# Quantised rows turned by VectorE and two transfers instead of TensorE, with each down product a tile later

## The chip, the cores and the metric

The kernel runs on one core of a Trainium2 chip. The metric is the device time of one execution in microseconds (us). TensorE is called PE in the profile, VectorE DVE, ScalarE ACT, GpSimd POOL and SyncE SP; PEld is PE's load of a stationary operand. Each engine works through its own instructions in order, and semaphores order the engines among each other.

## The reference, cut to what matters

A graph layer on 2500 nodes with 1024 features, followed by a feed-forward block whose rows and weights are quantised:

```
xn = layernorm(x)
x  = x + segment_sum((xn @ W)[src] * edge_weight, dst) + mix(xn)      # z of the kernel is x + mix(xn)
r  = layernorm(x)
x  = x + ffn(r)

ffn(r):  gate = silu(bitlinear(r, w_gate));  up = bitlinear(r, w_up)   # 1024 -> 512
         return bitlinear(gate * up, w_down)                           # 512 -> 1024
bitlinear(x, w) = act_quant(x) @ weight_quant(w).T
act_quant:    scale = 127 / max|row|;  clip(round(x * scale), -128, 127) / scale
weight_quant: scale = 1 / mean|w|;     clip(round(w * scale), -1, 1) / scale
```

The integers of a quantised row and the ternary weights are exact in bf16, so the feed-forward products are bf16 products, and the scales are multiplied in behind them.

## The kernel before, in words

The nodes lie in 20 tiles of 125 rows (`ROWS`, `TILES`). The early stages (layer norm, the mix branch, the dense adjacency matrix that GpSimd scatters in device memory, the support xn @ W) are not touched by the change. Two stages are.

**Aggregation** (PE from L1581, `sources` and `aggregate`). The sum over edges is a dense product A x S, done for a group of four node tiles at a time (`GROUPS` = 5 groups, `GT` = 4). All eight PSUM banks hold one group, two per tile. For each of 20 source tiles PE runs 24 products of 512 columns: each operand is split in a high and a low part, and three products are made of them (L366 to L368). ScalarE makes the high parts (L895, L898), VectorE the sum of the two halves of A and the low parts (L1215, L1220, L1222), in two pairs of buffers; SP loads the next slices of A when a buffer is free. A pair of sources is one turn of the loops (`high_of_pair`, `low_of_pair`).

While a group is summed, the group before it is finished in between: VectorE adds z (`add_z`), takes the rows' statistics, and quantises one tile in each of four consecutive pairs (`quantise_r`, L1257, in the work buffer `rc`, two halves used in turn). ScalarE turns the rounded values into bf16 integers (`integers`, L908), which before the change go to `rq16`, where all 20 tiles have a place. VectorE does not wait for that conversion until it needs the same half of `rc` again.

**Feed-forward** (PE from L1638). For each tile PE runs 16 products for gate and up (8 blocks of 128 features, each against 512 columns; `gate_up`, L1645), 4 transposes of the quantised hidden rows (`transpose_hidden`, L1658) and 8 down products (`down`, L1675). The gate and up products need the quantised rows with features on the partitions. Before the change PE makes this by 8 transposes per tile against an identity (`rows_across`, L1624), and ScalarE copies the result from PSUM to `rqT` (`transposed_x`, L942). For each tile ScalarE applies silu to the gate (L947), VectorE multiplies, finds the rows' largest value and rounds (`hidden`, L1319 to L1331), ScalarE makes integers (L953) and copies the transposed hidden rows from PSUM (L959), and VectorE adds the down product to the residual (`add_down`, L1345).

The order is written out by hand on each engine. `ffn_tile` of PE runs the gate and up products of tile t+1 with the hidden transposes of tile t among them, then the row transposes of tile t+2, then the down product of tile t. VectorE runs `hidden(t)` and then `add_down(t-1)`. The last group (tiles 16 to 19) is quantised inside this stage: its first half (`largest_r`) one tile ahead of those in `ROUNDED_AT` = (4, 6, 9, 12), its second (`round_r`) at them. SP loads r rows of the other 16 tiles back from device memory and writes the output.

Of the kernel before, what the change touches and what calls it, by code (L numbers as in the profile page):

```python
# [73 lines left out]
X_BANK = (0, 4)  # L74
# [29 lines left out]
def layer_kernel(nc, x, src, dst, edge_weight, W, Wq, bq, Wk, bk, Wv, bv, mix_w, w_gate, w_up, w_down, out):  # L104
# [8 lines left out]
    wT_d = nc.dram_tensor("ternary", (12, P, D), BF16).ap()  # L113

# [116 lines left out]
    rq16 = e3("rq16", [P, TILES, D], BF16)  # L231
# [4 lines left out]
    rqT = s6("rqT", [P, 2, KT, P], BF16)  # L236
# [29 lines left out]
    s_acc = sems("s_acc", GT)  # L266
# [47 lines left out]
    s_rtr = sems("s_rtr", 2)  # L314
# [98 lines left out]
    V_LOAD, V_TURN = KT, KT + 2  # L413

# [24 lines left out]
    def _(sp):  # L439
# [286 lines left out]
    def _(act):  # L726
# [181 lines left out]
        def integers(g, d):  # L908

            act.wait_ge(s_rq[d % 2], g * (GT // 2) + d // 2 + 1)  # L910
            nc.scalar.activation(rq16[0:ROWS, bass.ds(g * GT + d, 1), :].rearrange("p o n -> p (o n)"),
                                 rc[0:ROWS, d % 2, :], ACT.Identity, bias=neg_round[0:ROWS, :]).then_inc(s_rq16[d % 2], 1)
# [10 lines left out]
        with act.Fori(1, GROUPS) as g:  # L923
# [15 lines left out]
        def transposed_x(i, m, bank=6):  # L939
            act.wait_ge(s_rtr[i], m + 1)  # L940
            act.wait_ge(s_q[i], m)
            nc.scalar.activation(rqT[:, i, :, 0:ROWS], by_block(PS16[:, bank, :])[:, :, 0:ROWS], ACT.Copy).then_inc(s_rqT[i], 1)  # L942
# [7 lines left out]
        def ffn_tile(h, i):  # L950
# [4 lines left out]
            if h * 2 + i + 1 < TILES:  # L955
# [4 lines left out]
                                 PS16[:, 7, 0:512].rearrange("p (k n) -> p k n", k=4)[:, :, 0:ROWS],  # L960
                                 ACT.Copy).then_inc(s_xev[i], 1)
            if h * 2 + i + 3 < TILES:
                transposed_x(i, h + 1)

        nc.scalar.activation(norms[:, 7, 0:1], eps[:, :], ACT.Silu)
        transposed_x(0, 0, X_BANK[0])
        transposed_x(1, 0, X_BANK[1])
        act.wait_ge(s_fb, 1)
        silu_gate(0, 0, 0)
        for t in range(TILES):  # L970
# [3 lines left out]
            if t == TILES - 4:  # L974
                transposed_x(1, HALF - 1)
# [7 lines left out]
    def _(dve):  # L983
# [277 lines left out]
        def largest_r(g, d):  # L1261
# [3 lines left out]
            dve.wait_ge(s_rq16[i], g * (GT // 2) + d // 2)  # L1265
# [45 lines left out]
        def hidden(h, i, at=None):  # L1311

            t = h * 2 + i
            sc, hh = h_sc[0:ROWS, i if at is None else at, :], hid[0:ROWS, i, :]
# [18 lines left out]
        def add_down(t, bank=4):  # L1333

            h, i = divmod(t, 2)
            at = i if t + 1 < TILES else 2
# [22 lines left out]
        hidden(0, 0)  # L1359
# [14 lines left out]
        for t in range(TILES - GT - 2, TILES - 2):  # L1374
            hidden(t // 2, t % 2)
            add_down(t - 1)
        hidden(HALF - 1, 0)
        hidden(HALF - 1, 1, 2)
# [5 lines left out]
    def _(pe):  # L1384
# [196 lines left out]
        def sources(g, i, m, first, last_one, ends=False):  # L1581
# [5 lines left out]
            for d in ORDER:  # L1587
# [11 lines left out]
                if ends and d == ORDER[2]:  # L1599
                    for n in range(2):  # L1600
                        pe.wait_ge(s_rq16[n], (TILES - GT) // 2)
                    pe.wait_ge(s_r[ORDER[0]], GROUPS)
                    rows_across(0, 0, X_BANK[0])
            last.then_inc(s_pe5[i], 1)

        def aggregate(g, ends=False):
# [5 lines left out]
            for i in range(2):  # L1612
                sources(g, i, g * HALF + HALF - 1, False, i == 1, ends and i == 1)

        def transpose_x(t, i, m):
            if i == 0:
                pe.wait_ge(s_rqT[1], m)
            else:
                pe.wait_ge(s_rqT[0], m + 1)
            rows_across(t, i, 6)  # L1620

        def rows_across(t, i, bank):
            for k in range(KT):
                last = nc.tensor.transpose(PS16[:, bank, k * P:k * P + ROWS],  # L1624
                                           rq16[0:ROWS, bass.ds(t, 1), k * P:(k + 1) * P].rearrange("p o n -> p (o n)"),
                                           ident16[0:ROWS, 0:ROWS])
            last.then_inc(s_rtr[i], 1)

        aggregate(0)
        with pe.Fori(1, GROUPS - 1) as g:  # L1630
            aggregate(g)
        aggregate(GROUPS - 1, True)
# [5 lines left out]
        def gate_up(i, m, hidden_of=None):  # L1638
            pe.wait_ge(s_rqT[i], m + 1)
            pe.wait_ge(s_h[i], m)  # L1640
            for c in range(2):
                for k in range(KT):
                    if hidden_of is not None and c == 1 and k == KT // 2:
                        transpose_hidden(*hidden_of)
                    last = nc.tensor.matmul(PS[0:ROWS, 2 * i + c, :], rqT[:, i, k, 0:ROWS], wT[:, c, :, k * P:(k + 1) * P],  # L1645
# [83 lines left out]
```

## Time and profile before

| What | us |
|---|---|
| median of 3 runs (lowest, highest) | 1678.12 (1676.09, 1686.17) |
| the profiled execution | 1680.37 |
| its span, first to last instruction | 1678.6 |
| PE busy | 1653.2 (98%) |
| VectorE busy | 1095.4 (65%) |
| ScalarE busy | 519.1 (31%) |
| GpSimd busy | 588.5 (35%) |

The chain of waits that ended last has PE for 91% of the span, DMA for 5% and VectorE for 2%. The three aggregation product lines (L366 to L368, which also serve earlier stages) hold 23% each, the gate and up products (L1645) 4%, the down products (L1675) 2%, the transposes of quantised rows (L1624) 1%. The TensorE clock was granted at 0.998 of its full level over the span. Busy time of PE counts overlapping instructions once; how closely its products follow each other is read from start to start. Idle time of an engine off the chain costs nothing.

### The profile page before, as it was taken

The numbers are of one execution on the slowest core, as the hardware profiler recorded it, in microseconds if no ns is written. First come the engines' busy times: TensorE is split into PE (matmuls) and PEld (weight loads), VectorE is DVE, ScalarE is ACT, GpSimd is POOL, SyncE is SP. The second block draws the span as 40 slices with busy tenths as digits, with TensorE's granted clock in tenths as the row PEclk, the third lists the DMA queues.
The fourth block names the chain that finished last, engine by engine and source line by source line (L and its number), as shares of the span: only waits on it lengthen the run. The fifth ranks groups of instructions, "written<-read, shape, count | busy, mean of one in ns | idle before, by whom it ended". The sixth has DMA issues, their size and how long they took to land.

```text
span 1678.6 us, 23146 instructions
## 1 busy us (share of the span) xinstructions
PE 1653.2 (98%) x8036; PEld 1344.9 (80%) x8036; DVE 1095.4 (65%) x2548; ACT 519.1 (31%) x618; POOL 588.5 (35%) x392
## 2 busy tenths in 40 slices
PE   6999999999999999999999999999999999999998
PEld 5899999888888888888877777888788887887665
DVE  7866573576676876656666664476485674764886
ACT  4632210222222111114232222233333333332554
POOL 2011565777776777777677700000000000000000
PEclk9999999999999999999999999999999999999999
DMA  9999878655676755657877747345345345452454
GB/s 295 377 402 348 308 234 263 169 138 124 151 195 167 183 141 149 149 138 191 243 209 192 191 147 205 102 135 137 96 146 136 96 136 145 136 145 62 146 172 123
DMA packets 158003, 302.93 MB, mean 180 GB/s; under 512 B 60241, under 2 KB 95105, under 8 KB 157938
## 3 DMA queue, kind: packets, MB, share of 16 engines
q1 hardware_dynamic: 88302, 222.54, 42.2%
q0 software_dynamic: 61824, 52.62, 15.3%
q10 hardware_dynamic: 7812, 26.97, 5.3%
q8 instruction: 32, 0.52, 0.1%
q14 instruction: 33, 0.27, 0.1%
HBM read 202.88 MB, written 99.20 MB: 180 GB/s over the span
## 4 chain that ended last, share of the span: by engine, by line
PE 91%; DMA 5%; DVE 2%; issue 1%; ACT 1%; SPq 0%; DVEq 0%; ACTq 0%
PE PS L367 23%; PE PS L368 23%; PE PS L366 23%; PE PS L1408 4%; PE PS L1410 4%; PE PS L1409 4%; PE PS L1645 4%; DMA Aside<-A_dense 2%; PE PS L1675 2%; PE PS L1472 2%; DMA xnT<-XT 1%; DMA X<-in_x 1%; PE PS L1624 1%; DVE stats L995 1%; PE PS L1388 0%
## 5 line engine op out<-in xcount | busy, mean ns | idle before, releaser
L706 POOL DMA_INDIRECT A_dense<-wtot,cell x336 | 545.4, 1623 | 229.5 <-DMA A_dense<-wtot,cell 133.9
L367 PE MATMUL PS<-SH,AL 125*125 125x512 f32 x784 | 310.0, 395 | 0.0
L366 PE MATMUL PS<-SL,AH 125*125 125x512 f32 x784 | 308.4, 393 | 1.6 <-DVE AL L1222 1.4
L368 PE MATMUL PS<-SH,AH 125*125 125x512 f32 x784 | 309.8, 395 | 0.0
L366 PE MATMUL PS<-WL,xtH 128*125 128x512 f32 x640 | 252.9, 395 | 0.0
L367 PE MATMUL PS<-WH,xtL 128*125 128x512 f32 x640 | 252.0, 394 | 0.0
L368 PE MATMUL PS<-WH,xtH 128*125 128x512 f32 x640 | 251.6, 393 | 0.0
L1220 DVE TENSOR_TENSOR SL<-S,SH 125x1024 fp32r<-125x1024 f32 x98 | 119.9, 1223 | 166.1 <-ACT SH L895 166.1
L895 ACT ACTIVATE SH<-S 125x1024 fp32r (+1 forms) x98 | 103.9, 1061 | 316.4 <-PE PS L368 316.3
L366 PEld LDWEIGHTS PS<-SL,AH 125*125 125x125 f32 x784 | 145.9, 186 | 39.8 <-DVE AL L1222 3.1
L367 PEld LDWEIGHTS PS<-SH,AL 125*125 125x125 f32 x784 | 146.1, 186 | 36.0
L368 PEld LDWEIGHTS PS<-SH,AH 125*125 125x125 f32 x784 | 145.5, 186 | 34.5
L378 DVE SCALAR_TENSOR_TENSOR junk<-keyrow,key,ewrow 128x256 bf16<-128x256 f32 x336 | 149.0, 480 | 2.1 <-DMA ewrow<-weight_rows 1.8
L368 PEld LDWEIGHTS PS<-WH,xtH 128*125 128x125 f32 x640 | 118.9, 186 | 28.8
L366 PEld LDWEIGHTS PS<-WL,xtH 128*125 128x125 f32 x640 | 118.9, 186 | 28.4
L367 PEld LDWEIGHTS PS<-WH,xtL 128*125 128x125 f32 x640 | 119.0, 186 | 28.0
L366 PE MATMUL PS<-TL,xtH 128*125 128x512 f32 x320 | 126.7, 396 | 0.0
L367 PE MATMUL PS<-TH,xtL 128*125 128x512 f32 x320 | 126.7, 396 | 0.0
L368 PE MATMUL PS<-TH,xtH 128*125 128x512 f32 x320 | 126.2, 394 | 0.0
L1120 DVE TENSOR_TENSOR xtL<-xt,xtH 128x1000 fp32r<-128x1000 f32 x60 | 71.9, 1198 | 71.5 <-ACT xtH L826 71.2
L691 POOL DMA_DIRECT2D A_dense<-zeros x40 | 46.6, 1165 | 143.5 <-PE PS L1410 83.2
L1408 PE MATMUL PS<-ring 125*128 125x512 f32 (+4 forms) x260 | 90.3, 347 | 5.2 <-DVE ring L1012 5.2
(190 smaller groups left out, 2547.9 us busy)
## 6 DMA issues: line engine op xcount, KB each, us to landing
A_dense<-zeros POOLq DMA_DIRECT2D x40, 1280.0 KB, 8.3
xt<-xnT SPq DMA_DIRECT2D x60, 500.0 KB, 6.1
Araw<-A_dense SPq DMA_DIRECT2D x100, 250.0 KB, 2.7
Aside<-A_dense SPq DMA_DIRECT2D x100, 250.0 KB, 2.9
keyrow<-key_rows SPq DMA_DIRECT2D x42, 512.0 KB, 4.1
ewrow<-weight_rows SPq DMA_DIRECT2D x42, 512.0 KB, 5.6
xnT<-XT ACTq DMA_DIRECT2D x20, 500.0 KB, 10.2
zx<-in_x SPq DMA_DIRECT2D x20, 448.0 KB
```

The lines of the kernel that those rows point to most:

```text
L366: nc.tensor.matmul(o, lh, rl, start=start, stop=False)
L367: nc.tensor.matmul(o, ll, rh, start=False, stop=False)
L368: return nc.tensor.matmul(o, lh, rh, start=False, stop=stop)
L378: nc.vector.scalar_tensor_tensor(junk[:, slot, 2 * c:2 * c + 2, :].rearrange("p a n -> p (a n)"), row, key[:, col], wrow, ALU.is_equal, AL ...
L706: pool.indirect_dma_start(cells[m], bass.IndirectOffsetOnAxis(cell[:, col:col + 1], 0), wtot[:, col:col + 1], None, compute_op=ALU.add).th ...
L895: nc.scalar.activation(sh, S[0:ROWS, bass.ds(s, 1), :].rearrange("p o n -> p (o n)"), ACT.Copy).then_inc(s_s[i], 1)
L1120: nc.vector.tensor_tensor(xtL[i][:, :, :], xt[:, i], xtH[i][:, :, :].bitcast(F32), ALU.subtract).then_inc(s_xtl[i], 1)
L1220: nc.vector.tensor_tensor(sl, S[0:ROWS, bass.ds(s, 1), :].rearrange("p o n -> p (o n)"), sh.bitcast(F32), ALU.subtract)
L1408: nc.tensor.matmul(o, hi[:, cols], rl, start=first and opens, stop=False, skip_group_check=True)
L1409: nc.tensor.matmul(o, lo[:, cols], rh, start=False, stop=False, skip_group_check=True)
L1410: last = nc.tensor.matmul(o, hi[:, cols], rh, start=False, stop=last_one, skip_group_check=True)
L1645: last = nc.tensor.matmul(PS[0:ROWS, 2 * i + c, :], rqT[:, i, k, 0:ROWS], wT[:, c, :, k * P:(k + 1) * P], start=k == 0, stop=k == KT - 1)
```

## The change

The bf16 integers of a tile are written to the first half of the work buffer `rc` itself (`integer_rows`). VectorE transposes them in blocks of 32x32 into the second half (`turn_rows`, `turned_rows`), writing with a step of 8 elements. Four DMAs store the result to a new array in device memory, so that features get on its rows (`store_turned`, runs of 256 elements), and one DMA fetches it into `rqT`, which now holds all 20 tiles (`fetch_rows`). The transposes by PE, their PSUM banks and the copies by ScalarE are gone. The stationary operand of the gate and up products is read with a step of 8 elements and has 128 columns in place of 125.

For the first four groups the turning lies in the aggregation: VectorE turns a tile after the pair of sources that follows its quantisation, ScalarE's queue issues the stores a pair later, ahead of that pair's conversion, and the fetches another pair later. The next quantisation into the same half of `rc` waits for the store (`s_rqst`). For the last group VectorE turns inside the feed-forward stage, and SP issues the transfers between the output's writes.

In the feed-forward stage PE now runs: gate and up products of tile t, hidden transposes of tile t-1, down product of tile t-2. VectorE runs `hidden(t)` and `add_down(t-2)`; the scales of the hidden rows have three places.

```diff
+    rqT_d = nc.dram_tensor("rqT", (TILES, P, D), BF16).ap()
...
-    rq16 = e3("rq16", [P, TILES, D], BF16)
+    rqT = e3("rqT", [P, TILES, D], BF16)
...
+    def store_turned(eng, dram, rows, sem):
+        for a in range(4):
+            eng.dma_start(dram.rearrange("(b i) (a f) -> a i b f", b=4, a=4)[a],
+                          rows[a * 32:(a + 1) * 32, :].rearrange("p (b f) -> p b f", b=4)).then_inc(sem, 16)
+
+    def integer_rows(i):
+        return rc[:, i, 0:D // 2].bitcast(BF16)
+
+    def turned_rows(i):
+        return rc[:, i, D // 2:D].bitcast(BF16)
+
+    def store_rows(eng, g, d):
+        eng.wait_ge(s_turn, g * GT + d + 1)
+        store_turned(eng, rqT_d[bass.ds(g * GT + d, 1)].rearrange("o p n -> (o p) n"), turned_rows(d % 2), s_rqst[d % 2])
+
+    def fetch_rows(eng, g, d):
+        eng.wait_ge(s_rqst[d % 2], 64 * (g * (GT // 2) + d // 2 + 1))
+        eng.dma_start(rqT[:, bass.ds(g * GT + d, 1), :].rearrange("p o n -> p (o n)"),
+                      rqT_d[bass.ds(g * GT + d, 1)].rearrange("o p n -> (o p) n")).then_inc(s_rqT[d % 2], 16)
...
# SP, feed-forward
-        with sp.Fori(0, (TILES - GT) // 2 - 1) as h:
-            for i in range(2):
-                write_rows(h * 2 + i, h, i)
-                load_r(h * 2 + i + 2, i)
-        for t in range(TILES - GT - 2, TILES - 1):
+        for i in range(2):
+            sp.wait_ge(s_rqT[i], 16 * (TILES - GT) // 2)
+        for t in range(TILES - 1):
             write_rows(t, t // 2, t % 2)
+            if t + 2 < TILES - GT:
+                load_r(t + 2, t % 2)
+            if t + 1 in ROUNDED_AT:
+                store_rows(sp, GROUPS - 1, ROUNDED_AT.index(t + 1))
+            if t in ROUNDED_AT:
+                fetch_rows(sp, GROUPS - 1, ROUNDED_AT.index(t))
...
# ACT, aggregation
             for d in range(GT):
                 high_of_pair(g, 2 + d)
+                if d >= 1:
+                    store_rows(act, g - 1, d - 1)
                 integers(g - 1, d)
+                if d >= 2:
+                    fetch_rows(act, g - 1, d - 2)
...
-            with act.Fori(2 + GT, HALF) as h:
+            high_of_pair(g, 2 + GT)
+            store_rows(act, g - 1, GT - 1)
+            fetch_rows(act, g - 1, GT - 2)
+            high_of_pair(g, 3 + GT)
+            fetch_rows(act, g - 1, GT - 1)
+            with act.Fori(4 + GT, HALF) as h:
                 high_of_pair(g, h)
...
# DVE
-            dve.wait_ge(s_rq16[i], g * (GT // 2) + d // 2)
+            dve.wait_ge(s_rqst[i], 64 * (g * (GT // 2) + d // 2))
...
+        def turn_rows(g, d):
+            dve.wait_ge(s_rq16[d % 2], g * (GT // 2) + d // 2 + 1)
+            nc.vector.transpose(turned_rows(d % 2).rearrange("p (b j k) -> p b k j", b=4, j=32),
+                                integer_rows(d % 2).rearrange("p (k b j) -> p b k j", b=4, j=32)).then_inc(s_turn, 1)
...
+        nc.vector.memset(rc[96:P, :, :], 0.0)
...
             for d in range(GT):
                 quantise_r(g - 1, d)
                 low_of_pair(g, 2 + d)
+                turn_rows(g - 1, d)
...
         for t in range(1, TILES - GT - 2):
-            hidden(t // 2, t % 2)
-            add_down(t - 1)
+            hidden(t)
+            if t >= 2:
+                add_down(t - 2)
+            if t - 1 in ROUNDED_AT:
+                turn_rows(GROUPS - 1, ROUNDED_AT.index(t - 1))
...
# PE, feed-forward (ffn_tile, transpose_x and rows_across are removed)
-                    last = nc.tensor.matmul(PS[0:ROWS, 2 * i + c, :], rqT[:, i, k, 0:ROWS], wT[:, c, :, k * P:(k + 1) * P],
+                    last = nc.tensor.matmul(PS[:, 2 * i + c, :], rows[:, :, k], wT[:, c, :, k * P:(k + 1) * P],
...
+        gate_up(0, 0)
+        pe.wait_ge(s_r[1], GROUPS)
+        gate_up(1, 0)
+        for d in (2, 3):
             pe.wait_ge(s_r[d], GROUPS)
...
+        transpose_hidden(0, 0)
+        with pe.Fori(1, HALF) as h:
+            gate_up(0, h)
+            transpose_hidden(h - 1, 1)
+            pe.wait_ge(s_z[1], HALF + h - 1)
+            down(h - 1, 0, 4, False)
+            gate_up(1, h)
+            transpose_hidden(h, 0)
+            pe.wait_ge(s_z[0], HALF + h)
+            down(h - 1, 1, 4, False)
```

## Rows read from the trace of the kernel before

**Rows 1.** Windows: one aggregation group and the feed-forward stage (span; busy us of each engine with its count; clock; DMA).
```profile
core 0: us, PE busy (x) PEld busy (x) DVE busy (x) ACT busy (x) POOL busy (x), PEclk, DMA share, GB/s
1326.00:1438.00 112.00, 111.77 (x483) 89.40 (x482) 72.55 (x103) 39.46 (x47) 0.00 (x0) 1.00 0.44 128
1551.00:1660.00 109.00, 107.68 (x667) 71.50 (x665) 90.88 (x184) 61.47 (x80) 0.00 (x0) 1.00 0.51 151
```
**Rows 2.** Chain of waits, one tile of the feed-forward stage (start us, us, what).
```profile
1638.20 0.44 PE PS L1624 x8
1638.65 1.73 PE PS L1675 x8
1640.38 2.59 PE PS L1645 x12
...
1644.06 0.44 PE PS L1624 x8
```
**Rows 3.** Timeline of PE, start of the feed-forward stage (start, us, line; idle before).
```profile
1553.15 6.21 PE L1645 MATMUL PS<-wT,rqT 128*125 128x512 bf16 x28
1560.68 0.40 PE L1658 MATMUL PS<-ident,hq 125*128 125x125 bf16 x4 [1.32 <-ACT hq L953]
```
**Rows 4.** Timeline of VectorE (DVE), start of the feed-forward stage.
```profile
1554.04 2.46 DVE L1243 BATCH_NORM_STATS2 stats<-zr 125x6 f32<-125x512 f32 x4
1556.98 0.75 DVE L1319 SCALAR_TENSOR_TENSOR hid<-PS,u_back,gate 125x512 f32<-125x512 f32 x1 [0.48 <-PE PS L1645]
...
1562.74 0.70 DVE L1319 SCALAR_TENSOR_TENSOR hid<-PS,u_back,gate 125x512 f32<-125x512 f32 x1
```
**Rows 5.** Timeline of VectorE, feed-forward tiles that also quantise a last-group tile.
```profile
1577.86 0.80 DVE L1266 TENSOR_SCALAR rc<-zr,group_mv,rstd 125x1024 f32<-125x1024 f32 x1
...
1579.83 0.74 DVE L1319 SCALAR_TENSOR_TENSOR hid<-PS,u_back,gate 125x512 f32<-125x512 f32 x1
...
1582.64 1.28 DVE L1345 SCALAR_TENSOR_TENSOR fin<-PS,h_sc,rt 125x1024 f32<-125x1024 f32 x1
1583.83 0.14 DVE L1276 TENSOR_SCALAR x_back<-f_sc 125x1 f32<-125x1 f32 x1
...
1585.72 0.74 DVE L1319 SCALAR_TENSOR_TENSOR hid<-PS,u_back,gate 125x512 f32<-125x512 f32 x1
```
**Rows 6.** Timelines of PE and VectorE, the last tile's gate and up products.
```profile
1661.03 4.48 PE L1645 MATMUL PS<-wT,rqT 128*125 128x512 bf16 x20
...
1666.41 0.75 DVE L1319 SCALAR_TENSOR_TENSOR hid<-PS,u_back,gate 125x512 f32<-125x512 f32 x1 [1.36 <-ACT gate L947]
```
**Rows 7.** Timeline of VectorE, one quantising pair of the aggregation.
```profile
1472.82 0.67 DVE L1222 TENSOR_TENSOR AL<-Araw,AH 125x500 fp32r<-125x500 f32 x1
...
1477.31 0.81 DVE L1266 TENSOR_SCALAR rc<-zr,group_mv,rstd 125x1024 f32<-125x1024 f32 x1
...
1481.39 0.68 DVE L1215 TENSOR_TENSOR Araw<-Araw,Aside 125x500 f32<-125x500 f32 x1
...
1483.12 0.67 DVE L1222 TENSOR_TENSOR AL<-Araw,AH 125x500 fp32r<-125x500 f32 x1
```
**Rows 8.** Timeline of ScalarE (ACT), the same pair.
```profile
1474.49 1.06 ACT L895 ACTIVATE SH<-S 125x1024 fp32r<-125x1024 f32 x1 [2.07 <-PE PS L368]
...
1475.96 1.14 ACT L911 ACTIVATE rq<-rc,neg_round 125x1024 f32 x1
...
1485.62 1.06 ACT L895 ACTIVATE SH<-S 125x1024 fp32r<-125x1024 f32 x1 [2.89 <-PE PS L368]
```
**Rows 9.** Groups by line and shape, 1551 to 1679 us (count, busy us, mean ns; idle before).
```profile
L1645 PEld LDWEIGHTS PS<-wT,rqT 128*125 128x125 bf16 x320 | 42.4, 138 | 22.0
L1624 PEld LDWEIGHTS PS<-ident,rq 125*128 125x128 bf16 x61 | 3.9, 97 | 1.5 <-issue 0.3
L1269 DVE TENSOR_REDUCE f_sc<-rc 125x1 f32<-125x1024 f32 x4 | 4.9, 1220 | 0.1
```
**Rows 10.** DMA issues on ScalarE (L100, ns min/median/max), and landing of the ternary weights' stores (L600).
```profile
L100 ACTq DMA_DIRECT2D r<-zr x4: 342/350/396, 1119.1 to 1453.8; - x4
DMA to landing us min/median/max: 2.0/3.5/4.4
```

More of the change, by code:

```diff
@@ L73 @@
 NORM_BANK = (5, 1)
-X_BANK = (0, 4)
 ROUNDED_AT = (4, 6, 9, 12)
@@ L265, in layer_kernel @@
     s_Azero = sems("s_Azero", 2)
-    s_acc = sems("s_acc", GT)
+    s_acc = {d: sem(f"s_acc{d}") for d in (0, 2, 3)}
     s_bd = sem("s_bd")
@@ L313, in layer_kernel @@
     s_rstd = sem("s_rstd")
-    s_rtr = sems("s_rtr", 2)
+    s_rqst = sems("s_rqst", 2)
+    s_turn = sem("s_turn")
     s_s = sems("s_s", 2)
@@ L1309, in scales_back, with hidden @@
                                     ALU.mult).then_inc(s_fb, 1)
-        def hidden(h, i, at=None):
-            t = h * 2 + i
-            sc, hh = h_sc[0:ROWS, i if at is None else at, :], hid[0:ROWS, i, :]
+        def hidden(t):
+            h, i = divmod(t, 2)
+            sc, hh = h_sc[0:ROWS, t % 3, :], hid[0:ROWS, i, :]
             n = t * 5
@@ L1358, in _ @@
         dve.wait_ge(s_fb, 1)
-        hidden(0, 0)
+        hidden(0)
         row_stats(GROUPS - 1, ORDER[2:])
@@ L1373, in _ @@
         dve.wait_ge(s_fb, 2)
[L1374 to L1378, printed above, removed]
+        for t in range(TILES - GT - 2, TILES - 1):
+            hidden(t)
+            add_down(t - 2)
+        hidden(TILES - 1)
         for t, bank in ((TILES - 3, 4), (TILES - 2, 0), (TILES - 1, 2)):
@@ L1579, in _, with sources @@
         pe.wait_ge(s_fc, 3)
-        def sources(g, i, m, first, last_one, ends=False):
+        def sources(g, i, m, first, last_one):
             pe.wait_ge(s_lo5[i], m + 1)
@@ L1598, in sources, with aggregate @@
                     last.then_inc(s_acc[d], 1)
[L1599 to L1603, printed above, removed]
             last.then_inc(s_pe5[i], 1)
-        def aggregate(g, ends=False):
+        def aggregate(g):
             for i in range(2):
@@ L1612, in aggregate, with gate_up @@
             for i in range(2):
[L1613 to L1627, printed above, removed]
+                sources(g, i, g * HALF + HALF - 1, False, i == 1)
         aggregate(0)
-        with pe.Fori(1, GROUPS - 1) as g:
+        with pe.Fori(1, GROUPS) as g:
             aggregate(g)
-        aggregate(GROUPS - 1, True)
         def down_blocks(c, k):
             return wT[:, 2, 2 * c:2 * c + 2, :].rearrange("p a (b n) -> p (a b) n", b=2)[:, :, k * P:(k + 1) * P]
-        def gate_up(i, m, hidden_of=None):
-            pe.wait_ge(s_rqT[i], m + 1)
+        def gate_up(i, m):
+            rows = rqT[:, bass.ds(m * 2 + i, 1), :].rearrange("p o (r k) -> p (o r) k", k=KT)
+            pe.wait_ge(s_rqT[i], 16 * m + 16)
             pe.wait_ge(s_h[i], m)
@@ L1652, in transpose_hidden @@
             pe.wait_ge(s_hq16[i], h + 1)
[L1653 to L1656 removed]
+            pe.wait_ge(s_xev[i], HALF + h)
             for k in range(INNER // P):
[L1658 removed]
+                last = nc.tensor.transpose(PS16[:, 6 + i, k * P:k * P + ROWS], hq16[0:ROWS, i, k * P:(k + 1) * P],
                                            ident16[0:ROWS, 0:ROWS])
             last.then_inc(s_xtr[i], 1)
[L1662 to L1669 removed]
         def down(h, i, bank, by_halves):
@@ L1679, in down @@
             last.then_inc(s_u[i], 1)
-        pe.wait_ge(s_r[2], GROUPS)
-        rows_across(1, 1, X_BANK[1])
         pe.wait_ge(s_wT, 64)
+        pe.wait_ge(s_r[0], GROUPS)
         gate_up(0, 0)
-        for d in (1, 3):
+        pe.wait_ge(s_r[1], GROUPS)
+        gate_up(1, 0)
+        for d in (2, 3):
             pe.wait_ge(s_r[d], GROUPS)
-        ffn_tile(0, 0)
-        ffn_tile(0, 1)
-        with pe.Fori(1, (TILES - GT - 2) // 2) as h:
-            for i in range(2):
-                ffn_tile(h, i)
-        for t in range(TILES - GT - 2, TILES - 3):
-            pe.wait_ge(s_rq16[t % 2], (t + 2) // 2 + 1)
-            ffn_tile(t // 2, t % 2)
-        pe.wait_ge(s_rq16[1], HALF)
-        transpose_x(TILES - 1, 1, HALF - 1)
-        gate_up(0, HALF - 1, (HALF - 2, 1))
-        gate_up(1, HALF - 1)
-        transpose_hidden(HALF - 1, 0)
-        pe.wait_ge(s_z[0], 2 * HALF - 1)
-        down(HALF - 2, 1, 4, False)
+        transpose_hidden(0, 0)
[8 more added lines that the diff above has]
+            down(h - 1, 1, 4, False)
         pe.wait_ge(s_h[0], HALF)
```

34 lines of the change are left out of this document (4 added, 30 removed).

## The prediction

> **What bounds the kernel now.** I read the busy time by stretch first. In the aggregation of four node tiles (the second to fifth group look alike) PE is busy for all of the 112 us shown and VectorE for 73; in the feed-forward stage PE is busy for 107.7 of 109 us, but VectorE for 90.9 [rows 1]. The clock is at its full level in both, so PE's time is work, and VectorE is the engine with little left. The chain of waits through the feed-forward stage then gives PE's tile: 8 transposes of the quantised rows (0.44 us), the down product (1.73), 12 of the 16 gate and up products (2.59), the transposes of the hidden rows and the last four products; one tile to the next is 5.86 us [rows 2]. The timelines of VectorE and ScalarE at the edges of that stage and in one quantising pair of the aggregation [rows 3 to 8] show what stands ready when.
>
> **Part 1: PE's transposes leave the feed-forward stage.** 20 tiles x 0.44 us = 8.7 us off a chain that PE holds [rows 2]. The tile becomes 5.42 us. ScalarE's 20 evictions of the transposed rows go too; it had idle time, so they are worth nothing here.
>
> **Part 2: the start of that stage.** Now PE waits 1.32 us for the first hidden rows, 3.70 us after their VectorE chain starts at 1556.98 [rows 3, 4]. With the transposes gone the first products start 0.44 us earlier, at 1552.26 on an unchanged aggregation, and the first two tiles' products run to 1559.18. The first hidden chain can start when the row statistics end (1556.50 less 0.44, 1556.06), so PE waits to 1559.76: 0.58 us. Then come the third tile's products (3.46 us, to 1563.4). The second hidden chain started 5.76 us after the first [rows 4], so at 1561.8, and its transposes can run at 1565.5: a wait of 2.1 us, which the old order filled with the first down product. 2.7 against 1.3: +1.4 us.
>
> **Part 3: VectorE in that stage.** From row to row, a tile's hidden chain is 2.81 us and the addition of the down product 1.19, the first half of a last-group tile's quantisation 1.97, the second 1.89; in the old stage such tiles follow each other without a gap, at 5.89 us [rows 5]. The change adds one block transpose of 128x1024 in each of four tiles (5, 7, 10, 13). No row shows one. Ends: nothing (the start-to-start floor), and 2.4 us, twice a full-width pass; I take 1.2 us, the duration of the reduction over the same 1024 columns [rows 9]. Tiles 5 to 13 then need 9 x 4.00 + 3 x 1.97 + 3 x 1.89 + 4 x 1.2 = 52.4 us against PE's 9 x 5.42 = 48.8: +3.6 us. The looser order (the down product a tile later) gives slack for one tile, but a queue that is full for nine cannot be outwaited; the quieter tiles from 14 on catch up only up to PE. At the ends of the range of the transpose this term is 4.8 less (that is, none) and 4.8 more.
>
> **Part 4: the end.** The last tile's hidden chain starts 0.9 us after its products end, behind ScalarE's activation [rows 6]. In the new order the chain of the tile ahead begins a tile earlier, so this activation can start with the first half of the products: -0.7 us. What follows is untouched. The addition of tile 16, now between the last two hidden chains, takes 1.19 us of a stretch in which VectorE waits.
>
> Feed-forward stage: -8.7 + 1.4 + 3.6 - 0.7 = -4.4 us.
>
> **Part 5: the aggregation pays.** 16 tiles are turned there, in four groups, with PE full. In the pair shown PE gives up a source's buffers at 1474.5 and needs the refill of the other pair of buffers at 1485.6; two sources are 11.13 us [rows 8]. VectorE ends that pair at 1477.31, quantises for 4.08 us, and has the next source ready at 1481.39 + 2.40 = 1483.8: 1.8 us early [rows 7]. Now ScalarE issues four stores ahead of the conversion to integers, at 0.35 us each [rows 10]; with 0.3 us of them beside the activation in front (my choice), conversion moves from 1475.96 to about 1477.1 and ends at 1478.2. VectorE, which used to go straight on, waits 0.9 us for it, then turns the rows to 1479.5. The next quantisation also waits until the turned rows of two tiles before are stored, since they lie in the buffer that it overwrites. Those stores go out up to 1477.1. A store of 256 KB to device memory took 2.0 to 4.4 us, 3.5 in the median [rows 10]; the last quarter is smaller, and I take 2.6: 1479.7. Then 4.08 + 2.40: ready at 1486.2, 0.6 us late. Two pairs per group are so (third and fourth tile): 8 x 0.6 = 4.8 us. Before the second tile no store stands in the way; the row has 1.0 us of slack there (ready at 1473.5 [rows 7], needed at 1474.5), and 1.2 us of turning and 0.1 of hand-off make it 0.3 us late: 1.2 us over four groups. Together +6.0 us. Ends: nothing, if half a microsecond more is hidden; and with stores that take the row's 4.4 us, 1.8 us more in eight pairs, +20.4.
>
> **Edits that I cost at nothing.** The fetches (one issue and 256 KB each) and the 10 MB in all: the 16 DMA engines are half idle in both stages [rows 1], and a fetched tile has tens of microseconds until PE reads it; if that cover is gone, a fetch of a last-group tile would hold PE at tile 16 or later. In the last stage stores and fetches go through SP behind the output's writes and ahead of the next ones: up to nine issues of 0.35 us, 3.2 us of a 5.4 us tile; the row loads have a full tile of lead. One clearing of 32 partitions of the work buffer falls in the aggregation's first group, where VectorE waits. The wider products (128 rows in place of 125) stream the same 512 columns.
>
> **Part 6: the stationary operand.** Its columns now lie 16 bytes apart. The load is 0.138 us for 125 packed columns, and 0.097 for the 128-column loads of the transposes [rows 9], under products that follow each other at 0.216 us (12 in 2.59 [rows 2]). I take no cost, as it may grow by 0.08 us unseen. A gain has no room either: the spacing is the product's.
>
> **Where a rule speaks against it.** The Trainium skill, "SBUF — State Buffer", on cachelines: accesses that touch a new 16-byte line each time pay a penalty, and 8 bf16 is just that stride. No run here shows its size. "TensorE: Matmul & The Clock Gate", on weight-path modes, says that loads of 128 non-fp32 columns are read faster, packed or strided; the 0.097 against 0.138 us agrees for packed ones.
>
> **Sum.** -4.4 + 6.0 = +1.6 us. The profiled execution took 1680.37 us for a span of 1678.6; it would become 1682.0. It stands 2.25 us above the median of 1678.12, so on the median's scale 1679.7.
>
> **Rivals.**
> 1. *The turning is hidden in the aggregation.* Stores land within 2 us or issues overlap more. For it: 1.8 us of slack in each quantising pair. Against: three additions in series on VectorE. Only the feed-forward sum is left: 1678.1 - 4.4 = 1673.7; with a transpose of 0.7 us, 1671.7. Chance 0.20.
> 2. *Slower: the strided weight load shows.* It decides in the 320 gate and up loads, once one exceeds 0.216 us. At twice today's 0.138 us: 320 x 0.060 = 19.2 us; PE then sets the pace again, so the 3.6 us of part 3 vanish: -8.7 + 1.4 - 0.7 + 19.2 + 6.0 = +17.2, 1695.3. At three times: 320 x 0.198 = 63.4, 1739.5. From 0.275 us on it is slower by over 1%. For it: no load of the trace is strided. Against: 0.08 us of room, and the wide load is the shorter. Chance 0.10. By the cacheline sentence above it would be this case.
> 3. *The block transpose takes 2.4 us.* In the feed-forward stage +4.8; in the aggregation the turn ends at 1480.7 instead of the store's 1479.7, 8 x 1.0 = 8.0, and 4 x 1.2 = 4.8: 1679.7 + 17.6 = 1697.3. Against: the reduction of this width is 1.2 us. Chance 0.12. ("VectorE: DVE Perf Modes" of the Trainium skill, on the three transpose paths, gives 311 ns for 128x128, an estimate of 2.5 us for eight; with a fixed part in it, it would be less.)
> 4. *Stores land late,* 4.4 us or more after issue: the +20.4 above in place of 6.0, 1694.1 and up. Chance 0.08.
>
> **How the numbers follow.** My forecast has 0.50 (its own range 1674 to 1686). A change of under 1% (16.8 us) cannot be told from none here. Faster by over 1% would need twice all that PE gives up: 0.02. Slower: nearly all of rival 2 past its point 0.07, half of 3 (0.06), most of 4 (0.05), 0.02 for what I don't see: 0.20. The rest, 0.78, is no change. The range runs from rival 1's lower time, 1671, to rival 3's, 1697; beyond lie the worse half of rival 2 and a tenth of the rest.
>
> **What would show it.** Feed-forward: no transposes of quantised rows, tile spacing of 5.4 us outside tiles 5 to 13 and near 5.8 within, a wait of 2 us at the second hidden transposes. Aggregation: PE waiting for the low part of A, 0.3 to 0.6 us, three times a group. The block transpose at 1.2 us, and the gate and up products still 0.216 us apart. Wrong, if the aggregation shows no wait or one over 1 us each, or if the products spread.

## The result: 3.6% slower, 1740.1 us against 1677.1

The kernel after takes 1740.1 us in the median of 4 runs (1736.49 to 1741.18), the kernel before, run beside it, 1677.11 (1675.54 to 1686.17). The ratio is 1.0359 with a 95% interval of 1.0324 to 1.0393. The forecast was 1679.7 us in a range of 1671 to 1697, so time and range both missed. The profiled execution took 1736.49 us.

Windows of both kernels show where it went: the first stretch runs from the aggregation's first product to the first gate and up product, the second from there to the end of the span. First before, then after (columns as in [rows 1]).

```profile
992.20:1553.20 561.00, 558.43 (x2418) 446.71 (x2417) 341.67 (x468) 188.78 (x227) 0.00 (x0) 1.00 0.44 128
1553.20:1678.60 125.40, 117.14 (x707) 76.58 (x704) 98.61 (x201) 64.87 (x86) 0.00 (x0) 0.99 0.50 148
```
```profile
987.70:1598.00 610.30, 573.70 (x2402) 453.34 (x2400) 416.31 (x484) 189.17 (x226) 0.00 (x0) 0.97 0.45 131
1598.00:1734.80 136.80, 115.96 (x561) 73.11 (x560) 116.98 (x206) 45.47 (x67) 0.00 (x0) 0.96 0.52 150
```

The aggregation is 49.3 us longer, the feed-forward stage 11.4 us, where it should have been shorter. VectorE is 75 and 18 us busier, PE has 37 and 21 us without work where it had 3 and 8, and the granted clock fell from 1.00 to 0.97 and 0.96. The page names what is new on VectorE:

```profile
L1309 DVE STREAM_TRANSPOSE rc<-rc 128x1024 bf16<-128x1024 bf16 x20 | 96.6, 4828 | 19.7 <-ACT rc L935 19.7
```

One block transpose takes 4.83 us; the prediction had 1.2, and 2.4 as its upper end. The timeline of VectorE in a quantising pair of after answers [rows 7] (L1244 was L1222, L1237 was L1215, L1288 was L1266). The columns are start, duration and what ran; in brackets the idle time before.

```profile
1388.11 0.68 DVE L1244 TENSOR_TENSOR AL<-Araw,AH 125x500 fp32r<-125x500 f32 x1
1390.37 4.83 DVE L1309 STREAM_TRANSPOSE rc<-rc 128x1024 bf16<-128x1024 bf16 x1 [1.59 <-ACT rc L935]
1394.82 0.89 DVE L1288 TENSOR_SCALAR rc<-zr,group_mv,rstd 125x1024 f32<-125x1024 f32 x1
...
1398.99 0.67 DVE L1237 TENSOR_TENSOR Araw<-Araw,Aside 125x500 f32<-125x500 f32 x1
```

Between the end of one pair's low parts (1388.8) and the start of the next (1399.0) lie 10.2 us; in [rows 7] they are 4.1. PE's timeline in the same place:

```profile
1386.52 0.50 PE L366 MATMUL PS<-SL,AH 125*125 125x512 f32 x1 [3.67 <-DVE AL L1244]
1386.86 0.39 PE L367 MATMUL PS<-SH,AL 125*125 125x512 f32 x1
...
1388.40 0.63 PE L367 MATMUL PS<-SH,AL 125*125 125x512 f32 x1
1388.83 0.63 PE L368 MATMUL PS<-SH,AH 125*125 125x512 f32 x1
...
1391.39 0.44 PE L368 MATMUL PS<-SH,AH 125*125 125x512 f32 x1
1391.67 0.40 PE L366 MATMUL PS<-SL,AH 125*125 125x512 f32 x1
```

PE waits 3.67 us for the low part of A. After that wait its products, 0.23 us apart at first, are 0.43 us apart from 1388.40 to 1391.39: these seven steps take 1.4 us more than at the full clock. That is the level of 1.2 GHz in place of 2.4. The waits of PE in the whole aggregation:

```profile
PE PS L366 <- DVE AL L1244: 35.6, 14, 3.7
```

The kernel before has 1.4 us of them. Counted from start to start, eight stretches of slow products in the aggregation take 13.8 us more than at the full clock. The two are not independent. Here are the three waits of one group in after, and then the same three in e3_turns_agg, an experiment of below that turns as after does in this stage:

```profile
1263.62 0.50 PE L366 MATMUL PS<-SL,AH 125*125 125x512 f32 x1 [3.64 <-DVE AL L1244]
1278.56 0.59 PE L366 MATMUL PS<-SL,AH 125*125 125x512 f32 x1 [1.99 <-DVE AL L1244]
1293.57 0.50 PE L366 MATMUL PS<-SL,AH 125*125 125x512 f32 x1 [2.04 <-DVE AL L1244]
```
```profile
1263.39 0.50 PE L366 MATMUL PS<-SL,AH 125*125 125x512 f32 x1 [3.58 <-DVE AL L1244]
1278.31 0.50 PE L366 MATMUL PS<-SL,AH 125*125 125x512 f32 x1 [3.52 <-DVE AL L1244]
1293.40 0.50 PE L366 MATMUL PS<-SL,AH 125*125 125x512 f32 x1 [2.10 <-DVE AL L1244]
```

In after the first wait has a stretch of slow products behind it (1.6 us), and the second wait is 1.99 us. In e3_turns_agg the first wait has none, and the second is 3.52 us; that one has a stretch of 1.6 us behind it, and the third is 2.10. From wait to wait it is 14.9 to 15.1 us in both kernels and in all four groups. So VectorE sets the pace of these pairs, and what the lower clock takes is missing from the next wait. It lengthens the time only where no such wait follows, behind the last wait of a group: in the first and the last group of after, 1.6 and 2.5 us. From its first wait to the next group's, the first group takes 124.5 us, the second and third 122.9 and 123.3.

In the feed-forward stage, where VectorE turns the last group, it is the same (compare [rows 2] and [rows 5]):

```profile
1635.46 3.62 PE L1655 MATMUL PS<-wT,rqT 128*128 128x512 bf16 x16
1643.67 0.39 PE L1665 MATMUL PS<-ident,hq 125*128 125x125 bf16 x4 [4.59 <-ACT hq L981]
1644.11 3.58 PE L1673 MATMUL PS<-wT,hqT 128*125 128x512 bf16 x8
1647.53 3.62 PE L1655 MATMUL PS<-wT,rqT 128*128 128x512 bf16 x16
1650.98 0.39 PE L1665 MATMUL PS<-ident,hq 125*128 125x125 bf16 x4
1651.21 1.89 PE L1673 MATMUL PS<-wT,hqT 128*125 128x512 bf16 x8
```

The wait of 4.59 us follows the turning of the first last-group tile at 1633.48. The down product behind it takes 3.58 us instead of 1.89, again at half clock. In the whole stage PE waits seven times for the integers of the hidden rows, 14.2 us in all, and three down products are slow, by 4.2 us together. How much of these 4.2 us the next waits give back is not shown. Where VectorE is not turning, the tile is 5.41 us, as forecast.

### The profile page after: what moved, and what is told of

Same layout as the page of the kernel before. It is cut to its first block, busy times and chain, and to the rows that moved or that the text cites. A ratio compares the mean times of both kernels' runs of the same rounds, so it can differ in the third digit from the quotient of the medians.

```text
span 1734.8 us, 22971 instructions
## 1 busy us (share of the span) xinstructions
PE 1663.5 (96%) x7876; PEld 1343.5 (77%) x7876; DVE 1188.3 (68%) x2569; ACT 500.5 (29%) x598; POOL 585.4 (34%) x392
## 4 chain that ended last, share of the span: by engine, by line
PE 73%; DVE 15%; issue 6%; DMA 4%; ACT 2%; ACTq 1%; SPq 0%; DVEq 0%
PE PS L366 18%; PE PS L367 18%; PE PS L368 18%; PE PS L1439 4%; PE PS L1441 4%; PE PS L1440 4%; DMA Aside<-A_dense 3%; DVE SL L1242 2%; PE PS L1503 2%; DVE stats L1265 1%; DVE Araw L1237 1%; DVE AL L1244 1%; DVE rc L1309 1%; PE PS L1655 1%; DVE zr L1259 1%
## 5 line engine op out<-in xcount | busy, mean ns | idle before, releaser
L366 PE MATMUL PS<-SL,AH 125*125 125x512 f32 x784 | 314.4, 401 | 35.6 <-DVE AL L1244 35.6
L367 PE MATMUL PS<-SH,AL 125*125 125x512 f32 x784 | 314.9, 402 | 0.0
L368 PE MATMUL PS<-SH,AH 125*125 125x512 f32 x784 | 314.5, 401 | 0.0
L919 ACT ACTIVATE SH<-S 125x1024 fp32r<-125x1024 f32 (+1 forms) x98 | 103.7, 1058 | 284.8 <-PE PS L368 284.8
L1309 DVE STREAM_TRANSPOSE rc<-rc 128x1024 bf16<-128x1024 bf16 x20 | 96.6, 4828 | 19.7 <-ACT rc L935 19.7
L922 ACT ACTIVATE AH<-Araw 125x500 fp32r<-125x500 f32 x100 | 61.4, 614 | 117.7 <-DVE Araw L1237 117.7
```

The source lines that it names most:

```text
L366: nc.tensor.matmul(o, lh, rl, start=start, stop=False)
L367: nc.tensor.matmul(o, ll, rh, start=False, stop=False)
L368: return nc.tensor.matmul(o, lh, rh, start=False, stop=stop)
L919: nc.scalar.activation(sh, S[0:ROWS, bass.ds(s, 1), :].rearrange("p o n -> p (o n)"), ACT.Copy).then_inc(s_s[i], 1)
L1309: nc.vector.transpose(turned_rows(d % 2).rearrange("p (b j k) -> p b k j", b=4, j=32), integer_rows(d % 2).rearrange("p (k b j) -> p b k j ...
```

## The experiments

All comparisons are with the kernel before in the same session. The table gives the profiled execution of each by stretch (us): everything ahead of the aggregation, the aggregation, the feed-forward stage. No kernel touches the first column but for the order of the weights' columns in some; it still spreads over 4.5 us, more than any gain spoken of below, so small differences are judged by the ratios and by the other columns. In the kernel before, 0.9 us of row transposes lie inside the aggregation column.

| Kernel | one turn | ahead | aggregation | feed-forward | ratio to before (95%) |
|---|---|---|---|---|---|
| before | none | 992.2 | 561.0 | 125.4 | |
| after | 4.83 | 987.7 | 610.3 | 136.8 | 1.0359 (1.0324 to 1.0393) |
| e2_no_turns | 0.21 | 990.8 | 563.2 | 119.5 | 1.0000 (0.9982 to 1.0019) |
| e3_turns_agg | 4.83, 0.21 | 988.3 | 606.9 | 119.5 | 1.0265 (1.0245 to 1.0284) |
| e8_packed | 1.25 | 988.6 | 564.8 | 122.1 | 1.0002 (0.9987 to 1.0017) |
| e5_four | 1.10 | 988.3 | 562.0 | 121.1 | 0.9980 (0.9970 to 0.9990) |
| e7_twice | 2 x 1.10 | 989.1 | 575.7 | 125.6 | 1.0100 (1.0083 to 1.0117) |
| e9_old_order | 1.10 | 991.5 | 561.3 | 124.2 | 1.0016 (1.0005 to 1.0027) |
| e11_four_again | 1.10 | 990.4 | 562.2 | 121.2 | 0.9981 (0.9970 to 0.9992) |
| e10_convert_first | 1.10 | 987.9 | 561.1 | 121.1 | 0.9979 (0.9969 to 0.9990) |

**e1_forms: what makes the block transpose long.** Ten instructions behind VectorE's last one, each like these:

```diff
+        nc.vector.transpose(dst[:, 0:D].rearrange("p (b j k) -> p b k j", b=4, j=32),
+                            src.rearrange("p (k b j) -> p b k j", b=4, j=32)).then_inc(s_vtr, 1)
+        nc.vector.transpose(dst[:, 0:D].rearrange("p (b k j) -> p b k j", b=4, j=32), ...)
+        nc.vector.transpose(dst[:, 0:D], src)
```

> The kernel before, with ten extra instructions on VectorE behind its last addition, one after the other: the block transpose of 128x1024 bf16 in the change's form (output step of 16 bytes), with its blocks in the same order but packed output, flat, 128x128 flat, with output step of 4 bytes; of the same bytes as 128x512 four-byte elements flat, in packed blocks, and with output step of 16 bytes; then plain copies, packed and with the change's output step. Theory stride (the 16-byte step makes it long): the packed forms take 1.2 to 2.4 us against 4.83, the form with a step of 4 bytes lies between, the copy with the step is long as well. Rival width (a two-byte block transpose is that slow in any form): all 1024-element forms take 4.8 us, and the four-byte forms half of it, 2.4 us, as they have half the elements. Rival pattern (the four-dimensional access pattern costs): the flat form is short, the packed blocks are long. Total time of the kernel before plus the sum of the ten, 20 to 35 us.

Timeline of VectorE at its end. L1388 is the change's form, L1391 the same blocks packed, L1394 and L1396 flat, L1398 a step of 4 bytes, L1400 and L1402 four-byte elements flat and in packed blocks, L1405 four-byte elements with a step of 16 bytes, L1408 and L1410 copies, packed and with the change's output.

```profile
1677.20 4.70 DVE L1388 STREAM_TRANSPOSE rc<-rc 128x1024 bf16<-128x1024 bf16 x1
1681.94 1.25 DVE L1391 STREAM_TRANSPOSE rc<-rc 128x1024 bf16<-128x1024 bf16 x1
1683.22 1.25 DVE L1394 STREAM_TRANSPOSE rc<-rc 128x1024 bf16<-128x1024 bf16 x1
1684.50 0.31 DVE L1396 STREAM_TRANSPOSE rc<-rc 128x128 bf16<-128x128 bf16 x1
1684.85 1.31 DVE L1398 STREAM_TRANSPOSE rc<-rc 128x1024 bf16<-128x1024 bf16 x1
1686.20 0.71 DVE L1400 STREAM_TRANSPOSE rc<-rc 128x512 f32<-128x512 f32 x1
1686.94 0.71 DVE L1402 STREAM_TRANSPOSE rc<-rc 128x512 f32<-128x512 f32 x1
1687.69 1.08 DVE L1405 STREAM_TRANSPOSE rc<-rc 128x512 f32<-128x512 f32 x1
1688.81 0.43 DVE L1408 COPY rc<-rc 128x1024 bf16<-128x1024 bf16 x1
1689.27 2.43 DVE L1410 COPY rc<-rc 128x1024 bf16<-128x1024 bf16 x1
```

Same size, same type, same order of blocks on the input: 4.70 us with the output step of 16 bytes, 1.25 packed. So neither the transpose nor its four-dimensional pattern is slow, the step of the write is. As four-byte elements the same bytes with the same step of 16 bytes take 1.08 us. A copy with the change's access patterns pays as well, 2.43 us against 0.43 for a plain one. The kernel took 1693.7 us in one run, 15 us more than before with the ten instructions and a clearing; 20 to 35 us had been expected.

**e6_steps: from which step on.** The same place, flat input and one count, only the step differs.

> The kernel before with ten more forms at VectorE's end, now with one access pattern (flat input) and one count, so that only the output step differs: block transposes of 128x512 two-byte elements with output steps of 2, 4, 8 and 16 bytes, of 128x256 four-byte elements with steps of 4, 16 and 32 bytes, and copies with a step of 16 bytes and packed. Theory step (the write step in bytes sets the price, from a certain step on, for two-byte elements): packed 0.7 us, and 2.4 us at 16 bytes. If the price lies in the number of different 16-byte lines that the output touches, 8 bytes is cheap and 16 bytes dear, and four-byte elements at 16 and 32 bytes are dear alike. Rival pattern (the four-dimensional output, not its step, cost 4.7 us): the flat two-byte form with a step of 16 bytes takes 0.7 us too.

```profile
1676.10 0.71 DVE L1388 STREAM_TRANSPOSE rc<-zr 128x512 bf16<-128x512 bf16 x1
1676.85 0.75 DVE L1390 STREAM_TRANSPOSE rc<-zr 128x512 bf16<-128x512 bf16 x1
1677.63 1.31 DVE L1392 STREAM_TRANSPOSE rc<-zr 128x512 bf16<-128x512 bf16 x1
1678.97 2.44 DVE L1394 STREAM_TRANSPOSE rc<-zr 128x512 bf16<-128x512 bf16 x1
1681.45 0.45 DVE L1396 STREAM_TRANSPOSE rc<-zr 128x256 f32<-128x256 f32 x1
1681.93 0.63 DVE L1398 STREAM_TRANSPOSE rc<-zr 128x256 f32<-128x256 f32 x1
1682.59 0.64 DVE L1400 STREAM_TRANSPOSE rc<-zr 128x256 f32<-128x256 f32 x1
1683.26 1.30 DVE L1402 COPY rc<-zr 128x512 bf16<-128x512 bf16 x1
```

Two-byte elements at steps of 2, 4, 8 and 16 bytes take 0.71, 0.75, 1.31 and 2.44 us (L1388 to L1394): 8 bytes is dear already, 16 is 3.4 times packed. Four-byte elements at 4, 16 and 32 bytes take 0.45, 0.63 and 0.64 (L1396 to L1400): a mild price, and none beyond. The copy of two-byte elements at 16 bytes (L1402) takes 1.30: a copy pays for the step too, but the block transpose of the same size takes nearly twice as long. The theory that counts touched lines of 16 bytes fails as it was put on record, since it had 8 bytes cheap. The two-byte times do grow with the lines touched (128, 256 and 512 lines: 0.75, 1.31 and 2.44 us), but 256 four-byte elements on 256 lines take only 0.63, so the count of lines is not enough. What in VectorE makes it so stays open.

**e2_no_turns and e3_turns_agg: is it the length alone?** The block transposes cut short, all of them or only those of the last group; the stores then take the integer rows. These kernels leave out the turning of those tiles, and so do not compute the reference.

```diff
-            nc.vector.transpose(turned_rows(d % 2).rearrange(...), integer_rows(d % 2).rearrange(...)).then_inc(s_turn, 1)
+            nc.vector.transpose(turned_rows(d % 2)[:, 0:32], integer_rows(d % 2)[:, 0:32]).then_inc(s_turn, 1)
```

> The kernel after, with each block transpose cut to 128x32 (some 0.2 us) and the stores taken from the integer rows, so that all waits, conversions, stores, fetches and the new order stay and only the turning itself is left out (the feed-forward input is then not transposed). Theory length (the 4.8 us of VectorE, 20 times, and what they make PE wait for, are the whole loss): by the prediction's ledger with the transpose at nothing, -8.7 + 1.4 - 0.7 = -8.0 in the feed-forward stage and at most 4.8 in the aggregation, 1669 to 1674 us. Rival transfers (stores that land late, conversions behind issues, or contention cause a good part): 1690 us or more. Rival strided load: 1730 us, since its step is kept; the trace of after already speaks against it.

> The kernel after, with the four block transposes of the feed-forward stage cut to 128x32 and the 16 of the aggregation kept (the last four tiles' input is then not transposed). Theory length: the aggregation keeps its 45.5 us of loss and the feed-forward stage gains 8 us instead of losing 10.5, so about 1715 us. Rival (the feed-forward stage's new order costs by itself, or the aggregation's loss is caused elsewhere): 1725 us or more if the new order is to blame, 1740 if the four last transposes are hidden.

Without the turning the median is 1680.28 us (1670.51 to 1685.81, 10 runs) against 1678.53. All 62 us of the loss are gone, with every wait, conversion, store and fetch in place and the weight load's step kept: rivals transfers and strided load fall. But 1669 to 1674 was too low. The feed-forward stage did what was expected, 119.5 us. The aggregation, at 563.2, holds waits of VectorE for the stores:

```profile
PE PS L366 <- DVE AL L1244: 3.4, 2, 2.3
DVE rc L1288 <- DMA rqT<-rc: 3.3, 7, 0.8
```

The profiled execution is one of the shorter ones (1675.23), and why this kernel spreads over 15 us is open. With the turning in the aggregation alone the median is 1723.3 us: 606.9 us there and 119.5 in the feed-forward stage, so each stage pays for its own turns. 1715 had been expected; the profiled execution took 1716.39 at a clock of 0.993, the other three 5 to 10 us more at clocks of 0.986 to 0.991, which is not explained.

**e8_packed: one change, the output step.**

```diff
-            nc.vector.transpose(turned_rows(d % 2).rearrange("p (b j k) -> p b k j", b=4, j=32),
+            nc.vector.transpose(turned_rows(d % 2).rearrange("p (b k j) -> p b k j", b=4, j=32),
```

> The kernel after with one change: the block transpose writes its blocks packed (the same two-byte elements, same input, same size), while stores, fetches and the weight load's step stay; the features of a row then come in a wrong order, which leaves the arithmetic's amount as it is. Theory step: 1.25 us per transpose, and the time of the four-byte version, 1674 to 1679 us, since the 3.5 us of difference, 20 times, are the whole loss. Rival (two-byte transposes or the new transfers hurt in other ways): above 1690 us.

1677.9 us, ratio 1.0002, as expected: this one index order is the difference between 1740 and no change. The features of a row come in a wrong order here, so the kernel does not compute the reference; its amount of work is the same. The transpose takes 1.245 us, the price that the prediction had assumed, and the signs that the prediction named for it are there in small: PE waits nine times in the four groups for the low part of A, 0.2 to 0.3 us as a rule.

**e5_four and e11_four_again: the same step with four-byte elements.** The integers are turned in pairs; the gate and up weights are laid out to match, so the reference is computed.

```diff
+            nc.vector.transpose(rc[:, d % 2, D // 2:D].rearrange("p (b j k) -> p b k j", b=4, j=32),
+                                rc[:, d % 2, 0:D // 2].rearrange("p (k b j) -> p b k j", b=4, j=32)).then_inc(s_turn, 1)
...
+                    if pairs:
+                        block = fqb[:, i, :].rearrange("p (k c q) -> p k c q", k=4, q=2)[:, e // 2, :, e % 2]
```

> The kernel after, with the rows turned as pairs of bf16, 128x512 elements of four bytes, the output step 16 bytes as before; the weights' gate and up blocks take every second feature to match. It computes the reference. Theory element (cost goes by the element count): the transpose takes 2.4 us, and the ledger at 2.4 us gives 1677 + 1.6 + 17.6 = 1696 us. Rival byte (cost goes by bytes or by the step): 4.8 us and 1740 us unchanged. If the two-byte form alone is slow and four-byte elements move at one per cycle, 0.65 us: below the time of before, 1672 to 1678 us.

> The four-byte version unchanged, once more and in more rounds, to tell whether its gain over the kernel before is real: the first comparison gave a ratio of 0.998 with an interval of 0.997 to 0.999. Theory (PE's 8.7 us less 1.4 of start and what VectorE takes, 4.3 us of net gain in the feed-forward stage, 1 to 2 us lost in the aggregation): 2 to 4 us faster, ratio 0.9975 to 0.999. Rival (the first result was spread of the early stages, whose length differs by up to 4.5 us from profile to profile): ratio 1.000.

1675.26 and 1675.11 us, ratios 0.9980 and 0.9981, both intervals below 1: this version beats the kernel before by 3 us. Of the three cases expected for e5_four (1696 us, 1740 us, below 1678 us) the last came, though the turn is 1.10 us and not 0.65. VectorE's timeline in a quantising pair:

```profile
1362.01 0.67 DVE L1244 TENSOR_TENSOR AL<-Araw,AH 125x500 fp32r<-125x500 f32 x1
1363.62 1.12 DVE L1309 STREAM_TRANSPOSE rc<-rc 128x512 f32<-128x512 f32 x1 [0.94 <-ACT rc L935]
1364.56 0.75 DVE L1288 TENSOR_SCALAR rc<-zr,group_mv,rstd 125x1024 f32<-125x1024 f32 x1
...
1368.59 0.67 DVE L1237 TENSOR_TENSOR Araw<-Araw,Aside 125x500 f32<-125x500 f32 x1
```

The wait of 0.94 us for the conversion is as forecast (0.9). The quantisation starts without waiting for the store.

**e7_twice: the ledger at 2.3 us.** The four-byte version with each turn done twice.

> The four-byte version with every block transpose done twice, one after the other, so 2.3 us of VectorE in place of 1.1, and nothing else changed. Theory length: each of the 16 in the aggregation and 4 in the feed-forward stage adds 1.2 us to an engine that is full there: 4.8 us in the feed-forward stage and 5 to 14 us in the aggregation, 1685 to 1694 us. The prediction's rival 3 gave 1697 for 2.4 us. Rival slack (VectorE has room; only something beyond 4 us is felt): 1675 to 1679 us.

1693.63 us, ratio 1.0100. Against the four-byte version the aggregation grew by 13.7 us and the feed-forward stage by 4.5. The waits, and the clock over one of the four groups (it is 1.00 in the other three as well):

```profile
PE PS L366 <- DVE AL L1244: 14.6, 13, 1.5
```
```profile
1214.00:1326.00 112.00, 108.72 (x468) 86.06 (x467) 79.54 (x108) 39.29 (x47) 0.00 (x0) 1.00 0.49 142
```

PE waits 13 times, up to 1.5 us, and the clock stays at its full level: the waits are the whole growth here, with no slow products behind them. 1685 to 1694 us had been expected.

**e9_old_order: what the later down product is worth.** The four-byte version with hidden transposes inside the next tile's products, `down(t)` behind them and `add_down(t - 1)`.

```diff
+        def ffn_tile(h, i):
+            gate_up(1 - i, h + i, (h, i))
+            ...
+            down(h, i, 4, False)
```

> The four-byte version with the old order in the feed-forward stage: hidden transposes within the next tile's products, the down product of the same tile behind them, the addition one tile earlier; computes the reference. Theory order (the later down product is needed once PE's row transposes are gone, as PE's tile of 5.4 us no longer covers the chain from the products over VectorE and ScalarE to the down product): some 0.2 to 0.4 us a tile, less 1.4 us at the start, 1678 to 1682 us. Rival (the order is worth nothing, VectorE's load alone decides): 1674 to 1676 us.

1681.18 us, in the 1678 to 1682 expected; the feed-forward stage takes 124.2 us against 121.1. So the new order is worth 3 us there, once PE's row transposes no longer fill the tile. The ratios (1.0016 against 0.9980) lie 6 us apart; in the profiles the other 3 us against e5_four are ahead of the aggregation, where this edit changes nothing, and they are not explained.

**e10_convert_first: the last wait.**

```diff
-                if d >= 1:
-                    store_rows(act, g - 1, d - 1)
                 integers(g - 1, d)
+                if d >= 1:
+                    store_rows(act, g - 1, d - 1)
```

> The four-byte version with ScalarE's conversion ahead of the four stores in each pair, so that the turning no longer waits 0.9 us behind the issues (1.4 us) but the stores go out 1.1 us later. Theory issue (the 0.9 us wait is what still makes PE wait 0.2 us per pair, as VectorE is full there): 12 x 0.2 = 2.4 us less, ratio 0.9985 against the four-byte version. Rival (the later stores hold the next quantisation instead): no change or up to 2 us more.

1673.58 us, ratio 0.9979 to before. That is 1.5 us under e11_four_again beside it, where 2.4 had been expected, and no difference from the four-byte version that the intervals can tell. The aggregation column is 0.9 to 1.1 us shorter. The rival is seen as well: the wait for the conversion is gone and one for the stores has come in its place, 5.7 us in 8 waits.

```profile
DVE rc L1288 <- DMA rqT<-rc: 5.7, 8, 0.8
```

## Why the prediction was wrong, point by point

**The failed step is the price of the block transpose** in part 3 ("Ends: nothing, and 2.4 us, twice a full-width pass; I take 1.2 us"). It is 4.83 us. 1.2 us is right for the packed transpose (1.245 in e8_packed). The 16-byte step was in view, but it was weighed only for PE's weight load. The same step on VectorE's write, where it decides, was not listed, and the upper end was invented as "twice". Rival 3 named the right place with half the price. The prediction's own sign of being wrong came: waits of over 1 us each in the aggregation.

**The rest of the ledger holds when 4.8 us is put in.** Per turn 3.6 us more: 4 x 3.6 = 14.4 in the feed-forward stage, 8 x 3.4 = 27.2 and 4 x 3.6 = 14.4 in the aggregation; 1679.7 + 56.0 = 1735.7 us against 1740.1 measured. For 2.3 us (e7_twice) it gives 16 us more, 1695.7, against 1693.6. By stage: in the aggregation the ledger has 47.6 us (6.0 + 27.2 + 14.4), and after is 50.2 us longer there (610.3 against the 561.0 of before less its 0.9 of row transposes). A pair that also turns grows by 4.0 us in the ledger, from the 11.13 of [rows 8]; it measured 14.9 to 15.1. In the feed-forward stage it is 121.9 + 14.4 = 136.3 against 136.8. The clock, which no part had, is the smaller thing that it left out: 4.1 us in the aggregation, where most of the 13.8 us of slow products stand in for waiting, and at most 4.2 in the feed-forward stage.

**Part 1** is right: the transposes are gone and the tile is 5.41 us.

**Part 2** is right in kind. The first hidden transposes waited 0.66 us in after, forecast 0.58, the second 1.47, forecast 2.1. Its text has a slip: the start that it works with, 1552.26, is 0.9 us before the 1553.15 of [rows 3], two tiles' transposes and not the 0.44 it says.

**Parts 3 and 4, with a turn near 1.2 us:** forecast -4.4 us on a stage that begins 0.9 us earlier, that is 121.9; measured 121.1 (e5_four) and 122.1 (e8_packed).

**Part 5** was too high at 1.1 to 1.25 us: +6.0 forecast on 560.1 (561.0 less the 0.9 of row transposes), and +1.9 (e5_four), +4.7 (e8_packed) measured. The stores that I let hold the third and fourth tile did not: in e5_four the quantisation starts as the turn ends. It is not that they land sooner than the 2.6 us taken: in e5_four they took 2.2 to 6.8 us from issue to landing, 2.8 in the median. What the rows show is that wait and turn add 0.94 + 0.95 us there from start to start, against the 1.8 us of slack. Why the stores hold VectorE in e2_no_turns and e10_convert_first and not here is not settled. In after the wait for the conversion was longer than forecast, 1.6 us against 0.9.

**Part 6** is right in what it costs, and rival 2, a load that passes 0.216 us, is refuted. Its row (count, busy us, mean ns) in after's last stage, beside 138 ns in [rows 9]:

```profile
L1655 PEld LDWEIGHTS PS<-wT,rqT 128*128 x288 | 41.4, 144 | 21.2 <-issue 0.7
```

16 products still take 3.45 us from start to start. Against the 97 ns of 128 packed columns [rows 9] the load with the step is longer by half, but that was another operand, and no run loads these columns packed; 144 ns stay hidden in either case. So that rival 2 at three times today's load gives 1739.5 us, close to the measured time, is coincidence. Of the Trainium skill, "SBUF — State Buffer", the rule on cachelines (8 bf16 elements per 16-byte line) would make this load dearer; whether it did is open, and it cost no time. For VectorE's write the rule pointed the right way, but not at the right step: 8 bytes already costs 1.31 against 0.71 us.

**The chances.** The 0.20 for slower by over 1% was on the side that came, but the price was outside all cases, and so was the time.

## What to carry to other kernels

A new operation's price is bounded by its access pattern too, not only by its size: list the step in bytes of each operand, on each engine that touches the layout, and measure a form that the trace does not have before it goes on the path. A layout that needs a wide step is better written in four-byte than in two-byte elements: the same bytes and the same 16-byte step cost 4.7 us as bf16 and 1.1 us as pairs. Where an engine off the chain is nearly full, each microsecond given to it comes back on the chain almost whole (here 18.2 us in the two stages for 20 x 1.1 us more, e7_twice against e5_four). Long waits can take the clock with them, but slow work between two waits for the same engine is not lost twice: compare the spacing of the waits before adding the two up.

## What the runs showed of the hardware that I had not expected

- A block transpose on VectorE that writes bf16 with a step of 16 bytes takes 4.6 to 4.8 ns per element of a partition (2.44 us for 512, 4.70 for 1024), and packed 1.25 us for 1024. A plain packed copy of 1024 takes 0.43 us, and 2.43 with the change's output step and block order.
- The TensorE clock: behind waits of 1.9 to 4.6 us PE ran stretches at the 1.2 GHz level (products 0.43 us apart instead of 0.23), but not behind all of them. In the aggregation of after such a stretch followed each of the six waits of 3.6 to 3.7 us and two of the six of 2.0 to 2.1; in e3_turns_agg five of seven waits of 3.5 to 3.8 us and one of five of 1.9 to 2.1. What decides is not shown. The window from 1402 to 1406 us of after, behind a wait of 1.96 us, has a granted clock of 0.61. Behind waits of up to 1.5 us (e7_twice) the products kept the full pace.

```profile
1402.00:1406.00 4.00, 4.00 (x13) 0.61 0.81 229
1640.00:1644.00 4.00, 0.33 (x4) 1.00 0.14 34
1644.00:1648.00 4.00, 3.96 (x13) 0.57 0.71 190
```

These windows have PE's busy time, granted clock, DMA share and GB/s. In the second PE mostly waits, in the third it works at the lower level.
